# Border to the experts: spare entries written in advance, the last routing and the block table between the last chunks, one wait per producer

## The reference

```python
logits = x @ gate_w.T                       # 8 experts
topk_w, topk_i = jax.lax.top_k(softmax(logits), 2)
topk_w = topk_w / (topk_w.sum(-1, keepdims=True) + 1e-20) * 2.5
g = silu(einsum('td,edf->etf', x, w_gate)) * einsum('td,edf->etf', x, w_up)   # F = 352
y = einsum('te,etd->td', combine, einsum('etf,efd->etd', g, w_down))
return y + (silu(x @ sw_gate) * (x @ sw_up)) @ sw_down     # shared expert, width 704
```

## Time and profile before

| what | value |
|---|---|
| median of the timed runs | 1888.28 us (1886.03 to 1889.34) |
| span of the profiled execution | 1911.3 us |
| PE busy in it | 1755.3 us (92%) |
| DVE, ACT, POOL busy | 1257.1, 996.1, 931.6 us |
| first part of the experts, last step | about 1120 to 1146 us |
| border with no matmul on PE | 1146 to 1177.6 us |

### The profile page before, as it was taken

How to read it: one execution, slowest core, us unless ns; L and a number is a source line. 1 busy time by engine, 2 the same in 40 slices (tenths; PEclk the granted TensorE clock), 3 DMA queues, 4 the chain that set the end, 5 groups by cost and what they waited for, 6 DMA issues and landing times.

```text
span 1911.3 us, 41285 instructions
## 1 busy us (share of the span) xinstructions
PE 1755.3 (92%) x13058; PEld 1428.5 (75%) x13059; DVE 1257.1 (66%) x3093; ACT 996.1 (52%) x2315; POOL 931.6 (49%) x1115
## 2 busy tenths in 40 slices
PE   4999999999999999987999992999999999999997
PEld 3666666666666666656888882999999999987886
DVE  7778888888888888767556663433333333348787
ACT  2566676676767767663333332344444444435544
POOL 3455555555555555562576672455555555511101
PEclk8899999999999999997899996999999999999999
DMA  6655655566665555622532213223222222257775
GB/s 120 94 90 79 111 103 105 104 103 112 112 110 99 104 104 92 112 79 77 147 79 77 77 29 43 65 72 84 71 71 71 73 73 71 71 174 185 201 206 103
DMA packets 165317, 188.86 MB, mean 99 GB/s; under 512 B 43985, under 2 KB 123154, under 8 KB 165170
## 3 DMA queue, kind: packets, MB, share of 16 engines
q1 hardware_dynamic: 137794, 142.40, 36.0%
q0 software_dynamic: 25072, 43.67, 9.1%
q10 hardware_dynamic: 2304, 0.93, 0.3%
HBM read 85.00 MB, written 51.00 MB: 71 GB/s over the span
## 4 chain that ended last, share of the span: by engine, by line
PE 65%; DVE 9%; ACT 7%; issue 7%; POOL 4%; SPq 3%; another core or an unknown queue 2%; DMA 1%; ACTq 1%; POOLq 0%; DVEq 0%
PE bank L1617 5%; PE bank L2409 5%; PE bank L498 4%; PE bank L500 4%; PE bank L499 4%; PE bank L2411 4%; PE bank L2410 4%; PE bank L1674 4%; PE bank L1639 3%; PE bank L1619 3%; PE bank L1618 3%; ACT prob L1055 3%; PE bank L2430 2%; PE bank L1661 2%; PE bank L2432 2%
## 5 line engine op out<-in xcount | busy, mean ns | idle before, releaser
L916 POOL TENSOR_SCALAR_AFFINE_SELECT prob<-prob 128x512 f32<-128x512 f32 x256 | 163.4, 638 | 381.0 <-ACT prob L1055 380.8
L1055 ACT ACTIVATE prob<-bank 128x512 f32<-128x512 f32 (+1 forms) x512 | 249.0, 539 | 103.7 <-PE bank L1661 101.1
L2312 DVE TENSOR_TENSOR b_h<-b_h,bank 128x352 f32<-128x352 f32 x136 | 70.9, 521 | 300.5 <-ACT b_h L2260 251.4
L2239 POOL DMA_INDIRECT y_scratch<-b_y,names x136 | 135.6, 997 | 191.9 <-ACT b_y L2271 187.1
L1380 DVE COPY_PREDICATED bank<-from_prev,bank 128x512 f32<-128x512 int32 x192 | 133.1, 693 | 96.0 <-PE bank L1639 92.0
L1383 DVE TENSOR_REDUCE row_max<-bank 128x4 f32<-128x512 f32 x256 | 177.2, 692 | 25.9 <-PE bank L1639 18.4
L2409 PE MATMUL bank<-wgu_h,bxT_h 128*128 x544 | 184.1, 338 | 4.1 <-issue 3.0
L2411 PE MATMUL bank<-wgu_h,bxT_l 128*128 x544 | 176.0, 324 | 0.0
L2410 PE MATMUL bank<-wgu_l,bxT_h 128*128 x544 | 175.8, 323 | 0.0
L2260 ACT ACTIVATE b_h<-bank 128x352 f32<-128x352 f32 x136 | 63.2, 465 | 214.3 <-PE bank L2411 174.6
L2233 POOL DMA_INDIRECT bx<-xn_scratch,names x136 | 133.0, 978 | 77.3 <-issue 38.4
(11 more groups left out here) (349 smaller groups left out, 5244.5 us busy)
## 6 DMA issues: line engine op xcount, KB each, us to landing
kS<-qk_h SPq DMA_DIRECT2D x128, 128.0 KB, 4.0
qS<-qk_h SPq DMA_DIRECT2D x128, 128.0 KB, 5.8
f_y<-y_scratch SPq DMA_DIRECT2D x16, 1024.0 KB, 9.2
x_in<-in_L_attn_x_dram SPq DMA_DIRECT2D x16, 512.0 KB, 6.0
kS<-qk_l SPq DMA_DIRECT2D x64, 128.0 KB, 4.9
qS<-qk_l SPq DMA_DIRECT2D x64, 128.0 KB, 6.7
x_res<-in_L_attn_x_dram SPq DMA_DIRECT2D x16, 512.0 KB, 3.9
out_dram<-x_res SPq DMA_DIRECT2D x16, 512.0 KB, 5.0
```

The source lines that it names most:

```text
L916: op = e.affine_select(out=own, in_=own, compare_op=ALU.is_gt, fill=0.0, base=0, pattern=[[0, HG], [1, P]], channel_multiplier=-1)
L1055: e.activation(prob[:, u % SLOTS, 2 * hp:2 * hp + 2, 0:w], src[:, :, 0:w], ACT.Exp, scale=SCALE).then_inc(keyed.frees[hp], 1)
L2239: e.indirect_dma_start(out=y_dram, out_offset=bass.IndirectOffsetOnAxis(ap=b_names[:, b, 1:2], axis=0), in_=b_y[:, b % 2, :], in_offset=No ...
```

## The change

Six things are done, all around the border.

1. **Spare entries in advance.** Four `iota` on GpSimd (`spare_entries`, in the attention of sequence 2) fill all entries of all regions in SBUF; two transfers on SyncE (behind sequence 4's work) write them to `list_scratch`, in runs of 520 bytes. `base_p`, `spare_rows`, `spare_names` and the nine transfers at the border go. GpSimd waits for the two before its first scatter. `y_scratch` grows, since every spare entry now has a row of its own to write.
2. **Last step rewritten** (`last_step` on PE and DVE). `ranks("b")` moves ahead of step 6's last `shared_down`; "b" is placed and "a" chosen and placed around chunks 0 and 1; the work of `expert_blocks` is cut into four pieces that stand inside chunks 2 to 5.
3. **GpSimd's last step**: both scatters first, then the last two weight chunks. Chunk 15 has its own place in the arena, so its load needn't wait.
4. **One wait per producer.** `first_part_over` goes. SyncE waits for the table, reads four rows of it, then waits for the scatters; GpSimd waits for the last use of the hidden values (`h_used`); PE for table, weight chunks and the reads of its banks; ACT for each thing where it needs it.
5. **First names singly.** Groups of names are 1, 1, 2, 12, 40, 80 blocks, on three semaphores in turn. The store of the last `y_sb` is issued behind the names of block 3.
6. **Tables of ACT.** The exponentials of the router wait for the last `member` alone, and a small silu behind them brings the silu table.

```diff
@@ -842,8 +840,18 @@
+                def list_spare_rows():
+
+                    sp.wait_ge(spare_ready, 1)
+                    sp.dma_start(list_dram[0:E * REGION, :].rearrange("(x p j) a -> p x (j a)", x=E, p=P),
+                                 spare_list[:, :, :, :].rearrange("p x j a -> p x (j a)")).then_inc(spare_listed, 16)
+                    sp.dma_start(list_dram[E * REGION:, :].rearrange("(p j) a -> p (j a)", p=P),
+                                 spare_tail[:, :, :].rearrange("p j a -> p (j a)")).then_inc(spare_listed, 16)
                 for i in range(-1, SEQS - 1):
                     body(i, i % 2)
+                    if at(i, 4):
+                        list_spare_rows()
...
@@ -956,6 +964,15 @@
+                def spare_entries():
+
+                    run = REGION // P
+                    e.iota(spare_list[:, :, :, 0], pattern=[[0, E], [1, run]], base=0, channel_multiplier=run - 2)
+                    e.iota(spare_list[:, :, :, 1], pattern=[[REGION, E], [1, run]], base=2 * SEQS * S, channel_multiplier=run)
+                    e.iota(spare_tail[:, :, 0], pattern=[[1, SPARE]], base=0, channel_multiplier=SPARE)
+                    e.iota(spare_tail[:, :, 1], pattern=[[1, SPARE]], base=2 * SEQS * S + E * REGION, channel_multiplier=SPARE
+                           ).then_inc(spare_ready, 1)
...
@@ -982,6 +997,8 @@
+                        if at(i, 2) and u == 14:
+                            spare_entries()
...
@@ -1949,27 +1966,30 @@
+                LAST_CHUNK = 2 * T * D + C * S - 2 * F
+                assert 2 * NBLK * E <= LAST_CHUNK
+                def chunk_of(k):
+                    return chunk_in[:, :] if k < CHUNKS - 1 else arena[:, LAST_CHUNK:LAST_CHUNK + 2 * F]
+                def store_result(sp, m):
+                    for name in ("y0", "y1"):
+                        sp.wait_ge(*ys.read(m, name))
+                    sp.dma_start(ys_dram[m].rearrange("(t p) d -> p t d", p=P), y_sb[:, :, :]).then_inc(ys_stored, 16)
...
-                        reached(sp, stage_split, k)
                         x_, c = k // C, k % C
+                        if k < CHUNKS - 1:
+                            reached(sp, stage_split, k)
+                        else:
+                            sp.wait_ge(*small.filled(HALF - 1, "lga"))
-                    def list_spare_rows():
-
-                        sp.wait_ge(spare_ready, 1)
-                        with nc.allow_non_contiguous_dma(reason="a pair of numbers for each of 128 rows"):
-                            for x_ in range(E):
-                                row = sp.value_load(spare_rows[0:1, x_:x_ + 1], min_val=0, max_val=E * REGION)
-                                sp.dma_start(list_dram[bass.ds(row, P), :], spare_names[:, x_, :]).then_inc(spare_listed, 16)
-                            sp.dma_start(list_dram[E * REGION:, :].rearrange("(j p) a -> p j a", p=P), spare_names[:, E:, :]).then_inc(spare_listed, 16)
...
@@ -1985,11 +2005,8 @@
-                        if m == HALF - 1:
-                            list_spare_rows()
-                        for name in ("y0", "y1"):
-                            sp.wait_ge(*ys.read(m, name))
-                        sp.dma_start(ys_dram[m].rearrange("(t p) d -> p t d", p=P), y_sb[:, :, :]).then_inc(ys_stored, 16)
+                        if m < HALF - 1:
+                            store_result(sp, m)
...
@@ -2006,12 +2023,13 @@
-                        gp.wait_ge(stage_in, 32 * (k + 1))
-                        e.tensor_copy(hi, chunk_in[:, :]).then_inc(chunk_high, 1)
+                        gp.wait_ge(stage_in, 32 * (CHUNKS if k >= CHUNKS - 2 else k + 1))
+                        e.tensor_copy(hi, chunk_of(k)).then_inc(chunk_high, 1)
-                    for m in range(HALF):
+                        e.tensor_tensor(lo, chunk_of(k), hi.bitcast(f32), ALU.subtract).then_inc(stage_split, 1)
+
+                    gp.wait_ge(spare_listed, 32)
+                    for m in range(HALF - 1):
                         if m > 0:
                             split_chunk(2 * m)
                         scatter("b", m)
@@ -2021,6 +2039,10 @@
                         split_chunk(2 * m + 1)
                         if m > 0:
                             scatter("a", m)
+                    for kind in "ba":
+                        scatter(kind, HALF - 1)
+                    for k in (CHUNKS - 2, CHUNKS - 1):
+                        split_chunk(k)
 
...
@@ -2095,7 +2123,23 @@
-                    for m in range(HALF):
+                    def last_step(m):
+
+                        place(dve, "b", m)
+                        take_logits(dve, "a", m)
+                        hidden(dve, m, 0, h_f)
+                        choose_first(dve, "a", m)
+                        hidden_low(dve, m, 0, h_f, h_h, h_l)
+                        choose_second(dve, "a", m)
+                        hidden(dve, m, 1, h_f)
+                        place(dve, "a", m)
+                        hidden_low(dve, m, 1, h_f, h_h, h_l)
+                        for n, part in ((2, first_blocks), (3, experts_of_blocks), (4, rows_of_blocks), (5, finish_table)):
+                            hidden(dve, m, n, h_f)
+                            part()
+                            hidden_low(dve, m, n, h_f, h_h, h_l)
+
+                    for m in range(HALF - 1):
...
@@ -2123,7 +2164,7 @@
-                    expert_blocks()
+                    last_step(HALF - 1)
...
@@ -2142,7 +2183,20 @@
-                    for m in range(HALF):
+                    def last_step(m):
+
+                        gate_up(pe, m, 1, rT_h, rT_l)
+                        gate_up(pe, m, 2, rT_h, rT_l)
+                        ranks("a", m)
+                        count()
+                        shared_down(pe, m, 0, h_h, h_l)
+                        for n in range(3, FCS):
+                            gate_up(pe, m, n, rT_h, rT_l)
+                            shared_down(pe, m, n - 2, h_h, h_l)
+                        for n in (FCS - 2, FCS - 1):
+                            shared_down(pe, m, n, h_h, h_l)
@@ -2155,32 +2209,35 @@
-                        if m == HALF - 1:
-                            ranks("a", m)
                         gate_up(pe, m, 4, rT_h, rT_l)
-                        if m < HALF - 1:
-                            ranks("a", m)
+                        ranks("a", m)
...
-                        if m == HALF - 1:
-                            count()
...
+                        for c in range(C):
+                            pe.wait_ge(*small.read(m + 1, f"xT{c}a"))
+                        gate_up(pe, m + 1, 0, rT_h, rT_l)
+                        if m + 1 == HALF - 1:
+                            ranks("b", m + 1)
                         shared_down(pe, m, 5, h_h, h_l)
...
-            GROUPS = [range(0, 4), range(4, 16), range(16, 56), range(56, NBLK)]
-            names_in = [sem(f"names_in{n}") for n in range(len(GROUPS))]
+                    last_step(HALF - 1)
+            GROUPS = [range(0, 1), range(1, 2), range(2, 4), range(4, 16), range(16, 56), range(56, NBLK)]
+            LISTS = 3
+            names_in = [sem(f"names_in{n}") for n in range(LISTS)]
+            def names_landed(eng, n):
+
+                eng.wait_ge(names_in[n % LISTS], 16 * sum(len(GROUPS[j]) for j in range(n % LISTS, n + 1, LISTS)))
@@ -2189,31 +2246,37 @@
-                def first_part_over(eng):
-
-                    eng.wait_ge(ys_stored, 16 * HALF)
+                def lists_written(eng):
+
                     for kind in "ab":
                         for u in range(2):
                             eng.wait_ge(scattered[kind][u], 16 * 2 * T * (HALF // 2))
-                    eng.wait_ge(spare_listed, 16 * (E + 1))
-                    eng.wait_ge(stage_split, CHUNKS)
-                    eng.wait_ge(table_ready, 1)
...
-                    first_part_over(sp)
-
+                    EARLY = 4
+                    sp.wait_ge(table_ready, 1)
+                    def row_of(b):
+                        return sp.value_load(table[0:1, 0, b:b + 1], min_val=0, max_val=E * REGION + (SPARE - 1) * P)
+                    early = [row_of(b) for b in range(EARLY)]
+                    lists_written(sp)
...
+                    for n in range(len(GROUPS)):
+                        if n >= LISTS:
+                            names_landed(sp, n - LISTS)
+                        load_names(n)
+                        if n == 2:
+                            store_result(sp, HALF - 1)
+                        if n == 3:
@@ -2221,14 +2284,14 @@
-                    first_part_over(gp)
+                    gp.wait_ge(h_used, FCS * HALF)
@@ -2248,14 +2311,17 @@
-                    first_part_over(act)
-                    e.activation(probs, lg_all[:, :, :], ACT.Exp).then_inc(exp_ready, 1)
+                    act.wait_ge(member_ready, 2 * HALF)
+                    e.activation(probs, lg_all[:, :, :], ACT.Exp)
```

(18 more changed lines are left out.)

62 lines of the change are left out of this document (24 added, 38 removed).

## The result

The changed kernel takes 1867.93 us (median; 1866.35 to 1868.33), the kernel before 1888.65 us (1886.03 to 1889.34). The ratio is 0.9889, with a 95% interval of 0.9875 to 0.9903: 20.7 us faster. The forecast was 1867.2, in a range of 1863 to 1874.

A forecast was written before the change was run, and what follows sets the result against it. The border before the expert loop was taken as a chain of five serial waits, none needing PE. Border gain 21.9 less 0.5 (block 4) and 0.3 (attention) gives 21.1, so 1888.28 becomes 1867.2 us, range 1863 to 1874.

The forecast's parts named there:

- table done: DVE's last table operation in the last step: 22.9 us of work from `hidden`, ending at 1147.2 against 1154.84.
- PE's last matmul: Last `shared_down` on PE at about 1149, some 3 us later than before, off the path.
- lists landed: Last scatter landing 1 to 3 us behind its end on GpSimd: 1145 to 1149.
- first names: SyncE issues block 0's names at 1150.2, after four table reads taking 3.0 us.
- first gather: GpSimd's gather for block 0 at 1152.7, 2.5 us behind its names.
- first turn: PE's first turn of rows at 1155.7, 3.0 us behind the gather, 21.9 us earlier than before.
- block 4 and attention: Block 4's gather lands late, 0.5 us lost; iotas delay a select in attention, 0.3 us lost.
- I assume that this border is not stretched by it: Profiled span, 23.0 us above the median, leaves the border's length alone; stretched by 1.2% it would be 0.3 us.
- The store does hold the gather: Rival at the first gather: its signal waits for the `y_sb` store; gain 1.3 to 7.4 smaller, 1868.5 to 1874.6; 0.17.
- The lists or PE come last: Rival at the border: these, not the table, end last; first names 2 to 4 us later, 1869 to 1871; 0.17.
- The clock: PE's clock falls in the gap, no gain counted; rival: stays 1.00, 1866 to 1867; 0.04 with other small gains.
- the table's move: Table work moved between the last step's chunks on DVE: 7.6 us of the border's 21.9.

## Why the prediction was right, step by step

Measured against its own anchor (the gate before is at 1123.27, so its `hidden` of 1124.3 is 1.0 behind the gate, and so on):

| step | predicted, behind the gate | measured | why the difference |
|---|---|---|---|
| `hidden` of chunk 0 | 1.0 | 1.7 | `place` of "b" and `take_logits` stand ahead of it on DVE; I had counted only PE's ranks |
| table done | 23.9 | 24.8 | 0.7 from the anchor; 1.2 from GpSimd, less 1.0 elsewhere |
| PE's last matmul | 25.7 | 29.1 | GpSimd's splits beside `hidden_low`; 25.6 without them |
| lists landed | 21.7 to 25.7 | about 28 | landing takes 4 us, not 1 to 3; the first scatter starts 0.9 us behind the latest time I allowed; three scatters of 1.5 us |
| first names | 26.9 | 28.0 | follows from both |
| first gather | 29.4 | 31.1 | 3.1 us from the names, not 2.5 |
| first turn | 32.4 | 34.3 | 3.3 us from the gather, not 3.0: the store, issued 0.7 us ahead of it |
| block 4 and attention | 0.5 + 0.3 lost | nothing found | see below |

*What held.* The border was one chain, and the steps went where the forecast put them. The table's stretch, the largest term, was 22.9 us predicted and 23.1 measured from `hidden` to its end, partly by two errors that cancel. The prices that were too low add up along the chain: 0.9 us late at the table, 1.0 at the names, 1.7 at the gather, 1.9 at the first turn, which comes 20.0 us earlier than in the first profile instead of 21.9. Against it, the 0.8 us counted as lost in attention and at block 4 were not lost. So the path was right, but that the total came within 0.7 us of the median is in part luck: the first turn alone gives 19.7 to 20.4 us where 21.9 were forecast. The four iotas took 0.62, 0.60, 0.14 and 0.14 us, not up to 3.9, and the spare list landed in 6.8 us with the next loads of `x_in` at 301.81 and 351.41 for 300.18 and 350.84: 1.6 us late once, 0.6 the next time, and within 0.3 us from then on. Block 4's gather is 14.8 us behind the first (before 13.4), and PE turns its rows without a wait.

*What was wrong but did no harm.* "I assume that this border is not stretched by it" was right, but the reason for the high span was not profiling: that one execution lost 21 us further ahead. The prediction was safe only because it took the gain from the border and set it off against the median, not span from span.

*Rivals.* The store does hold the gather, but by 0.2 to 0.3 us and not by the rival's 1.3 to 7.4: it lands in 2.9 us, not in 5.5 or 11.6, and the gather's own 3.0 us hide most of that. The Trainium skill's "DMA: Bandwidth & Descriptors", section "Queues, rings and completion order", was the ground for that rival. A delay that grows to 0.6 us as the store comes nearer agrees with its rule in direction, but does not show it; a longer store was not tried. "The lists or PE come last" is half true: the lists come in at the same moment as the table's reads. The clock was at its lower level in the hole, as counted.

*Shares.* At the first turn: 54.7 before, 43.8 with the spare entries alone, 34.3 to 34.6 with everything. The remaining 9.4 are no sum of parts. With the table moved but one wait for all it is 41.7, with separate waits but the table behind 44.9, no better than without either; together they bring 9.4. The forecast gave the table's move 7.6 as a share of its own; it is worth 2.1 us at most while everything waits for the store, and 10.5 once nothing does (about 2.8 of these are the operations that GpSimd's splits hold up when the table stands beside them). Not undone alone, and so without a share: the scatters ahead of GpSimd's last splits, and the order of ACT's tables.

## What to carry to other kernels

Read a border as a chain of waits and price each link, but expect that removing the last arrival shows the next one: spare writes, then scatters, then store and table, then lists. Two edits that shorten parallel arrivals pay only together, so undo each alone before giving it a share. When an idle gap is to be filled, ask first which engines the awaited transfer itself needs: here GpSimd had to write the gather, and DVE in the gap held it up. Take a span from one profiled execution only beside a second one of the same kernel.

## What the runs showed of the hardware

- DVE and GpSimd hold each other up. A DVE operation with two operands in SBUF, or a copy or cast there, that meets a GpSimd split does not get through until the split is over: 0.17 us became 1.32 and 1.52, ending with the split; a `hidden_low` of 0.69 became 2.18, ending 0.55 behind it (and 0.69 again with the splits away), and the next split then took 1.24 instead of 0.77. The recorded spans are not exact here: the cast that took 0.82 instead of 0.22 ended inside the first split, 0.21 behind its recorded start.
- The reverse holds for indirect transfers: three scatters of 1.48, 1.60 and 1.50 us and the gather of 2.68 each end 0.83 to 0.85 us behind the end of a DVE `tensor_tensor` between SBUF operands (the gather: 1137.83, behind 1137.00), where undisturbed ones take 0.95 to 1.0. (The third scatter: 1124.38, behind 1123.53 of the `tensor_tensor` at 1122.26.) In all of them but one the `tensor_tensor` was running when the transfer started; in the second scatter it began 0.09 us behind the start. Not every overlap does it: the scatter at 1124.68, with a `tensor_tensor` beginning 0.19 us behind it, took its usual 0.96, and with the spares only two that start within 0.02 us of one took 0.97. The Trainium skill, "SBUF — State Buffer", section "Who interferes with whom", states an exclusive lock on the ports that DVE and GpSimd share, held for the whole instruction where DVE uses both pairs for one tensor, and that a DVE instruction with two SBUF inputs contends with a GpSimd instruction that reads SBUF; the times above agree. By what it marks as inferred, `tensor_tensor` takes only the read side and would not hold a descriptor's writing, and here it held the transfer: the measurement decides. Whether the descriptors or the reading of the transfer's offsets from SBUF waited, no run tells.
- A scatter of 128 pairs lands about 4 us after its 0.97 us on GpSimd; names of 1 KB land in 1.7 us at best, and the first gather starts 2.5 to 3.6 behind the issue of names that have a semaphore value of their own; a gather of 128 rows of 1 KB takes 2.9 to 3.1 from issue to PE, and up to 3.6 with a 512 KB store issued just ahead.
- 3.9 us of back-to-back matmuls, begun at the lower clock 1.3 us after PE's last real one, did not bring the clock back, nor did they keep block 0 from running at 1.2 GHz; it rose 4.7 us behind block 0's first gate matmul, in the changed kernel without filler 3.3 us behind it. The kernel before starts its loop at the lower clock too (0.50 at 1182 to 1184).
